# Norm stage of a four-layer kernel: turned pairs go round four PSUM banks in place of two, and ScalarE evacuates five of the eight pairs

## The chip, the cores and the metric

One NeuronCore of a Trainium2 chip. The metric is the device time of one execution in microseconds (us). Engines are called PE (TensorE, with its weight loads PEld), DVE (VectorE), ACT (ScalarE), POOL (GpSimd) and SP (SyncE, here the queue that issues most DMAs).

## What is computed

Two transformer layers on x of shape (2, 1024, 256), 2048 tokens in all, each sublayer behind a layer norm and with a residual:

```python
x = x + L0_attn(layernorm(x))      # 16 heads of 16, rotary embedding, causal
x = x + L0_ffn(layernorm(x))       # own norm with ln_weight, ln_bias; then @ sign(weight).T * max|weight| * gamma + beta
x = x + L1_attn(layernorm(x))      # 16 heads of 128, biases, causal
x = x + L1_ffn(layernorm(x))       # 64 experts, top 6 of 3 groups, capacity 96, plus a shared expert

def _layernorm(x, axis=-1, eps=1e-05):
    m = jnp.mean(x, axis=axis, keepdims=True)
    v = jnp.var(x, axis=axis, keepdims=True)
    return (x - m) / jnp.sqrt(v + eps)
```

The second norm is applied twice (the plain one and that of the feed-forward layer), in one pass.

## The kernel before, in words

The kernel is written by hand, engine by engine. x stays in SBUF as 16 tiles of 128 tokens x 256 (`g.x`). The program is a row of blocks. In a block each engine has its own list of instructions in the order written, semaphores join them, and a barrier of all engines ends the block: the next block begins when the last engine is through, SP's waits for its loads and stores included.

Four of these blocks are made by `norm` (line 164), one ahead of each sublayer:

- n0, ahead of the first attention. SP loads weights for the stages behind it.
- n1 (kind "ffn"), with a second level of statistics; its evacuation multiplies by `lnw` and adds `lnb`. No DMA.
- n2 (kind "split"), ahead of the second attention. The result is wanted as two f16 parts whose sum is the value: ScalarE copies the bank to `g.xs[0]` (line 274), VectorE subtracts that from the bank to `g.xs[1]` (line 257). SP loads 2.9 MB of weights.
- n3 (kind "keep"), ahead of the experts. SP also stores the normalized rows to DRAM (line 305).

Each norm has the same skeleton. VectorE computes mean and 1/std of all tiles in a chain of small operations, with one square root on ScalarE. Then it normalizes the 16 tiles one by one (line 249, 16 operations in 5.3 us) and signals each (`s_xn`). PE turns the tiles in eight pairs: a pair is two tiles of 128 tokens, and gives four 128x128 transposes (line 288) into one bank, of which the pair fills 512 f32 columns. A pair is then evacuated by two operations of 128x256 into the feature-major tensor `g.xT` (or `g.xs`). PE reuses a bank only when a semaphore says that it is empty.

Before the change the banks and the evacuating engines alternate together: pair p goes to bank p % 2, even pairs are evacuated by ScalarE (lines 202, 205), odd ones by VectorE (lines 197, 200). VectorE's evacuations stand behind its sixteen normalizing operations in its list. In n2 both engines work on every pair, and VectorE's subtraction frees the bank. PE waits so:

```python
for p in range(NT // 2):
    pe.wait_ge(s_xn, N0 + 2 * p + 2)
    if p >= 2:
        pe.wait_ge(s_ev[p % 2], N0 // 4 + p // 2)
```

The blocks behind the norms are: `l0_qkv` (line 371), where VectorE takes the maximum of a weight (`absmax`, line 334), POOL reduces it over the partitions (line 338) and then does an addition for each tile (line 441); `l0_ffn` (matmuls of line 1303); the second attention; and the router with the shared expert (matmuls of lines 1512 and 1525), whose SP queue begins the load of the expert weights.

Of the kernel before, what the change touches and what calls it, by code (L numbers as in the profile page):

```python
# [30 lines left out]
ACT = mybir.ActivationFunctionType  # L31
# [3 lines left out]
P = 128  # L35
B, S, D = 2, 1024, 256
T = B * S
NT = T // P
# [122 lines left out]
                dve.wait_ge(s_v, 3)  # L161


def norm(nc, g, tag, kind, loads=None, pool_work=None):


# [4 lines left out]

    s_sq, s_ch = [g.sem(f"{tag}_{n}") for n in ("sqrt", "chain")]
    s_st, s_ag, s_xn, s_tr = [g.sem(f"n_{n}") for n in ("stats", "aggr", "xn", "tr")]
    s_ev = [g.sem(f"n_evac{i}") for i in range(2)]

    N0 = int(tag[1]) * NT
    s_hi = g.sem(f"{tag}_hi") if kind == "split" else None
    s_kept = g.sem(f"{tag}_stored") if kind == "keep" else None
    with ExitStack() as c:
# [8 lines left out]
        with nc.Block() as block:  # L188
            def evac(eng, p):

                eng.wait_ge(s_tr, N0 // 2 + p + 1)
                for c_ in range(DC):
                    src = g.bank[p % 2][:, 0, c_ * 256:(c_ + 1) * 256]
                    dst = g.xT[:, c_, p * 256:(p + 1) * 256]
                    if p % 2:
                        if kind == "ffn":
                            ins = eng.tensor_scalar(dst, src, g.lnw[:, c_:c_ + 1], g.lnb[:, c_:c_ + 1],
                                                    ALU.mult, ALU.add)
                        else:
                            ins = eng.tensor_copy(dst, src)  # L200
                    elif kind == "ffn":
                        ins = eng.activation(dst, src, ACT.Identity, bias=g.lnb[:, c_:c_ + 1],
                                             scale=g.lnw[:, c_:c_ + 1])
                    else:
                        ins = eng.activation(dst, src, ACT.Copy)
                ins.then_inc(s_ev[p % 2], 1)

            @block.vector
            def _(dve):
                n = 0  # L210

                def chained(ins):

                    nonlocal n
                    n += 1
                    ins.then_inc(s_ch, 1)
                    dve.wait_ge(s_ch, n)

                if tag == "n0":
                    for t in range(NT):  # L220
                        dve.bn_stats(st[:, t, :], g.x[:, t, :]).then_inc(s_st, 1)
                for t in range(NT):
                    if tag == "n0":
                        dve.wait_ge(s_st, N0 + t + 1)
                    dve.bn_aggr(mv[:, t, :], st[:, t, :]).then_inc(s_ag, 1)
                dve.wait_ge(s_ag, N0 + NT)
                chained(dve.tensor_copy(g.mean[:, :], mv[:, :, 0]))
                chained(dve.tensor_copy(t1, mv[:, :, 1]))
                for lv in range(levels):
                    chained(dve.tensor_scalar(ve, t1, EPS, None, ALU.add))  # L230

                    dve.wait_ge(s_sq, lv + 1)
                    chained(dve.reciprocal(sq[:, :], sq[:, :]))
                    r = g.rstd[:, :]
                    one = sq[:, :]
                    chained(dve.tensor_tensor(t1, one, one, ALU.mult))
                    chained(dve.tensor_tensor(t1, t1, ve, ALU.mult))
                    chained(dve.tensor_scalar(t1, t1, -0.5, 1.5, ALU.mult, ALU.add))
                    if lv == 0:
                        chained(dve.tensor_tensor(r, one, t1, ALU.mult))  # L240
                    else:
                        chained(dve.tensor_tensor(one, one, t1, ALU.mult))
                        chained(dve.tensor_tensor(r, r, one, ALU.mult))
                    if lv + 1 < levels:

                        chained(dve.tensor_tensor(t1, r, r, ALU.mult))
                        chained(dve.tensor_tensor(t1, t1, mv[:, :, 1], ALU.mult))
                for t in range(NT):
                    dve.tensor_scalar(xn[:, t, :], g.x[:, t, :], g.mean[:, t:t + 1], g.rstd[:, t:t + 1],
                                      ALU.subtract, ALU.mult).then_inc(s_xn, 1)  # L250
                if kind == "split":
                    for p in range(NT // 2):

                        dve.wait_ge(s_hi, DC * (p + 1))
                        for c_ in range(DC):
                            cols = slice(p * 256, (p + 1) * 256)
                            ins = dve.tensor_tensor(g.xs[1][:, c_, cols], g.bank[p % 2][:, 0, c_ * 256:(c_ + 1) * 256],
                                                    g.xs[0][:, c_, cols], ALU.subtract)
                        ins.then_inc(s_ev[p % 2], 1)
                else:  # L260
                    for p in range(1, NT // 2, 2):
                        evac(dve, p)

            @block.scalar
            def _(act):
                for lv in range(levels):

                    act.wait_ge(s_ch, 3 if lv == 0 else 11)
                    act.activation(sq[:, :], ve, ACT.Sqrt).then_inc(s_sq, 1)
                if kind == "split":  # L270
                    for p in range(NT // 2):
                        act.wait_ge(s_tr, N0 // 2 + p + 1)
                        for c_ in range(DC):
                            act.activation(g.xs[0][:, c_, p * 256:(p + 1) * 256],
                                           g.bank[p % 2][:, 0, c_ * 256:(c_ + 1) * 256], ACT.Copy).then_inc(s_hi, 1)
                else:
                    for p in range(0, NT // 2, 2):
                        evac(act, p)

            @block.tensor  # L280
            def _(pe):
                for p in range(NT // 2):
                    pe.wait_ge(s_xn, N0 + 2 * p + 2)
                    if p >= 2:
                        pe.wait_ge(s_ev[p % 2], N0 // 4 + p // 2)
                    for c_ in range(DC):
                        for j in range(2):
                            ins = pe.transpose(g.bank[p % 2][:, 0, (2 * c_ + j) * P:(2 * c_ + j + 1) * P],
                                               xn[:, 2 * p + j, c_ * P:(c_ + 1) * P], g.identf[:, :])
                    ins.then_inc(s_tr, 1)  # L290

# [1742 lines left out]
```

## Time and profile before

| | us |
|---|---|
| median of 3 runs | 1579.84 |
| lowest, highest | 1574.81, 1579.88 |
| the profiled execution's own time | 1579.99 |
| its span in the trace | 1578.3 |

| engine | busy us | share of the span |
|---|---|---|
| PE | 1407.0 | 89% |
| DVE | 1050.9 | 67% |
| PEld | 985.8 | 62% |
| ACT | 813.1 | 52% |
| POOL | 375.3 | 24% |

The shares are averages over stages with different limits. The two attentions (96 to 382 us and 475.7 to 1240 us) keep PE nearly always busy; the norms lie between stages, at 10.9 to 31.5, 422 to 439, 457 to 475.4 and 1240 to 1255 us, and there no engine is busy all the time. How a stage is limited is read from its own rows, and in the norms from what the transposes wait for.

### The profile page before, as it was taken

To read this page: it belongs to the slowest core of one execution; us is meant where nothing else is said; L and a number is where in the kernel's file an instruction comes from. 1 tells how busy PE (TensorE), PEld (TensorE's weight loads), DVE (VectorE), ACT (ScalarE), POOL (GpSimd) and SP (SyncE) were. 2 spreads that over 40 slices of the span, in tenths; PEclk is the share of its full clock that TensorE was granted. 3 is DMA by queue.
4 is the path that set the end of the run, shared out by engine and by line. 5 is a ranking of instruction groups with operands and counts; after the bars stand their busy time and mean duration, and the time that the engine had idled before them with its cause. 6 is when DMAs were issued, how large, how long until landed. Compare 5 with 4: busy or idle time off the path is not lost. (4 is left out here: it accounts for less than half of the span.)

```text
span 1578.3 us, 36418 instructions
## 1 busy us (share of the span) xinstructions
PE 1407.0 (89%) x12869; PEld 985.8 (62%) x12869; DVE 1050.9 (67%) x2197; ACT 813.1 (52%) x1676; POOL 375.3 (24%) x796
## 2 busy tenths in 40 slices
PE   3848999998669999999979999999998798699977
PEld 2414555454555777777767677777777645599953
DVE  4766777775766888888841888888882368522229
ACT  1215656556216777777730787777781115333330
POOL 0344656430020111111120111111101000477730
PEclk9968999999869999999999999999999789799985
DMA  3027999972023755556540566556652340599948
GB/s 100 1 59 158 243 250 240 212 170 54 1 77 77 139 134 137 133 136 139 136 91 1 112 138 140 135 133 140 140 122 44 106 118 0 141 290 300 283 131 291
DMA packets 463402, 215.08 MB, mean 136 GB/s; under 512 B 412083, under 2 KB 434449, under 8 KB 463073
## 3 DMA queue, kind: packets, MB, share of 16 engines
q1 hardware_dynamic: 448992, 175.09, 46.9%
q0 software_dynamic: 12000, 36.90, 7.9%
q10 hardware_dynamic: 2336, 2.16, 0.4%
q8 instruction: 39, 0.64, 0.2%
q14 instruction: 35, 0.28, 0.1%
HBM read 81.97 MB, written 31.52 MB: 72 GB/s over the span
## 5 line engine op out<-in xcount | busy, mean ns | idle before, releaser
L1055 PE MATMUL bank<-a_pt,v_part 128*128 128x128 f16 x3456 | 234.2, 219 | 14.9 <-DMA a_pt<-a_ph 9.5
L737 DVE TENSOR_REDUCE a_qh<-bank 128x1 f16<-128x1024 f32 (+7 forms) x256 | 182.3, 755 | 86.5 <-PE bank L627 84.9
L1118 ACT ACTIVATE a_ph<-a_p,a_rinv 128x1024 f16<-128x1024 f32 (+7 forms) x256 | 198.6, 777 | 79.0 <-POOL a_rinv L997 76.0
L1055 PEld LDWEIGHTS bank<-a_pt,v_part 128*128 128x128 f16 x3456 | 207.7, 98 | 48.4 <-DMA a_pt<-a_ph 7.8
L1126 DVE TENSOR_REDUCE a_negm<-bank 128x1 f32<-128x1024 f32 (+7 forms) x256 | 191.8, 750 | 55.9 <-PE bank L1039 55.7
L1034 PE MATMUL bank<-a_k,a_q 128*128 128x512 f16 (+3 forms) x1152 | 228.6, 326 | 0.2
L725 ACT ACTIVATE a_p<-bank 128x1024 f32<-128x1024 f32 (+7 forms) x256 | 158.0, 650 | 129.8 <-PE bank L682 113.8
L1160 DVE SCALAR_TENSOR_TENSOR a_ph<-a_p,a_rinv,a_ph 128x1024 f16<-128x1024 f32 (+7 forms) x256 | 206.9, 808 | 1.7 <-ACT a_ph L1118 1.7
L1107 ACT ACTIVATE a_p<-bank,a_negm 128x1024 f32<-128x1024 f32 (+7 forms) x256 | 189.5, 740 | 21.6 <-DVE a_negm L1126 21.5
L997 POOL TENSOR_TENSOR a_rinv<-a_rinv,p_scale 128x1 f32<-128x1 f32 x256 | 49.0, 191 | 615.4 <-DVE a_rinv L1139 615.2
L906 PE MATMUL bank<-x_part,wsplit 128*128 128x512 f16 x768 | 187.3, 381 | 4.0 <-PEq L188 1.8
L624 PE MATMUL bank<-a_k,a_q 128*128 128x512 f16 (+3 forms) x384 | 109.5, 342 | 33.8 <-DMA a_k<-a_kh 19.4
L1034 PEld LDWEIGHTS bank<-a_k,a_q 128*128 128x128 f16 x1152 | 99.4, 98 | 60.6 <-ACT a_p L1107 1.2
L682 PE MATMUL bank<-a_qm,a_k 128*128 128x512 f16 (+3 forms) x384 | 113.0, 333 | 6.6 <-ACT a_p L725 5.2
L906 PEld LDWEIGHTS bank<-x_part,wsplit 128*128 128x128 f16 x768 | 70.1, 98 | 72.2 <-issue 5.6
L1742 POOL DMA_INDIRECT x_rows<-token_rows,src x64 | 63.1, 986 | 172.6 <-issue 170.2
L1793 PE MATMUL bank<-x_T,wgu 128*88 128x96 f32 x1024 | 96.4, 248 | 0.7 <-issue 0.7
L915 PE MATMUL bank<-wsplit,x_part 128*128 128x128 f16 x1536 | 95.9, 219 | 0.8 <-DVE a_k L941 0.5
L1793 PEld LDWEIGHTS bank<-x_T,wgu 128*88 128x88 f32 x1024 | 92.9, 158 | 4.5 <-issue 1.0
L915 PEld LDWEIGHTS bank<-wsplit,x_part 128*128 128x128 f16 x1536 | 88.2, 98 | 5.7 <-DVE a_k L941 2.1
L1911 DVE TENSOR_TENSOR x_h<-bank,x_sg 88x192 f32<-88x192 f32 x64 | 22.6, 354 | 94.8 <-ACT x_sg L1870 94.8
L1188 PE MATMUL bank<-wo_part,z_part 128*128 128x256 f16 x768 | 84.2, 273 | 1.7 <-PEq L966 1.7
(206 smaller groups left out, 2246.4 us busy)
## 6 DMA issues: line engine op xcount, KB each, us to landing
wgu<-in_wgu SPq DMA_DIRECT2D x64, 352.0 KB
choice_rows<-zero POOLq DMA_DIRECT2D x24, 512.0 KB, 5.2
c_rows<-choice_rows SPq DMA_DIRECT2D x16, 768.0 KB, 11.5
wsplit<-w_parts POOLq DMA_DIRECT2D x30, 384.0 KB, 3.9
wd<-in_wd SPq DMA_DIRECT2D x64, 176.0 KB
pw_in<-in_wqkv SPq DMA_DIRECT2D x16, 384.0 KB, 5.3
w_parts<-pw_part SPq DMA_DIRECT2D x16, 384.0 KB, 2.9
a_pt<-a_ph SPq DMA_TRANSPOSE x256, 3.0
```

What stands on the lines that cost most here:

```text
L682: ins = pe.matmul(ST[k % 2][:, c4 * 512:c4 * 512 + w_], kT[s][:, kb, :], queries[:, kb * P + c4 * 512:kb * P + c4 * 512 + w_], start=True, ...
L725: act.activation(pT[s][:, off[kb]:off[kb + 1]], ST[k % 2][:, 0:(BT - kb) * P], ACT.Exp).then_inc(e_ready, 1)
L737: dve.tensor_reduce(qh[s][:, i, MC:MC + 1], s1_place(t), AX.X, ALU.max, negate=True).then_inc(m_ready, 1)
L906: ins = pe.matmul(G_ps[k % 2], w[:, a, c_, (k // 2) * P:(k // 2 + 1) * P], g.xs[x_][:, c_, b * S + (k % 2) * 512:b * S + (k % 2 + 1) * 512 ...
L915: ins = pe.matmul(G_ps[k % 2][:, j * P:(j + 1) * P], g.xs[x_][:, c_, t * P:(t + 1) * P], w[:, a, c_, 2 * P:3 * P], start=(c_ == 0 and (a, ...
L1034: ins = eng.matmul(ps[:, c4 * 512:c4 * 512 + w_], qT[par][a][:, i * P:(i + 1) * P], kT[par][k_][:, c4 * 512:c4 * 512 + w_], start=(a, k_) ...
L1055: ins = eng.matmul(Z_ps[:, cols], g.vs[par][v_][:, k, :], turned[slot][:, a * blocks[j] + k, :], start=(k == 0 and (v_, a) == PARTS[0]), s ...
L1107: eng.activation(probs[j % NBUF][:, 0:w_], S_ps[j % 4][:, 0:w_], ACT.Exp, bias=negm[:, par, j:j + 1], accum_out=rsum[:, par, j:j + 1]).the ...
L1118: eng.activation(parts[slot][:, 0:w_], probs[slot][:, 0:w_], ACT.Copy, scale=rinv[:, p_, jj:jj + 1]).then_inc(p_hi, 1)
L1126: eng.tensor_reduce(negm[:, par, j:j + 1], S_ps[j % 4][:, 0:blocks[j] * P], AX.X, ALU.max, negate=True).then_inc(m_ready, 1)
L1160: eng.scalar_tensor_tensor(parts[slot][:, w_:2 * w_], probs[slot][:, 0:w_], rinv[:, p_, jj:jj + 1], parts[slot][:, 0:w_], ALU.mult, ALU.su ...
L1793: ins = pe.matmul(b_[:, m * C:(m + 1) * C], g.wgu[s][:, c_, m * MH:(m + 1) * MH], xeT[(s // 2) % 2][:, s % 2, c_, :], start=(c_ == 0), sto ...
```

## The change

`BY_DVE` lists the pairs that VectorE evacuates: 3, 5 and 7. ScalarE takes 0, 1, 2, 4 and 6. Pair p goes to bank p % 4. The semaphores `s_ev` now count by engine (0 ScalarE, 1 VectorE) and not by bank, and PE waits from pair 4 on, for the evacuation of pair p - 4. In the split norm both engines still work on every pair, and only the banks change.

```diff
@@ -161,6 +161,10 @@
                 dve.wait_ge(s_v, 3)
 
 
+BY_DVE = (3, 5, 7)
+
+
 def norm(nc, g, tag, kind, loads=None, pool_work=None):
 
 
@@ -171,9 +175,16 @@
 
     s_sq, s_ch = [g.sem(f"{tag}_{n}") for n in ("sqrt", "chain")]
     s_st, s_ag, s_xn, s_tr = [g.sem(f"n_{n}") for n in ("stats", "aggr", "xn", "tr")]
+
     s_ev = [g.sem(f"n_evac{i}") for i in range(2)]
 
     N0 = int(tag[1]) * NT
+    def earlier_norms(by):
+
+        each = len(BY_DVE) if by else NT // 2 - len(BY_DVE)
+        halves = 1 if int(tag[1]) == 3 else 0
+        return each * (int(tag[1]) - halves) + halves * by * (NT // 2)
+
     s_hi = g.sem(f"{tag}_hi") if kind == "split" else None
     s_kept = g.sem(f"{tag}_stored") if kind == "keep" else None
     with ExitStack() as c:
@@ -190,9 +201,9 @@
 
                 eng.wait_ge(s_tr, N0 // 2 + p + 1)
                 for c_ in range(DC):
-                    src = g.bank[p % 2][:, 0, c_ * 256:(c_ + 1) * 256]
+                    src = g.bank[p % 4][:, 0, c_ * 256:(c_ + 1) * 256]
                     dst = g.xT[:, c_, p * 256:(p + 1) * 256]
-                    if p % 2:
+                    if p in BY_DVE:
                         if kind == "ffn":
                             ins = eng.tensor_scalar(dst, src, g.lnw[:, c_:c_ + 1], g.lnb[:, c_:c_ + 1],
                                                     ALU.mult, ALU.add)
@@ -203,7 +214,13 @@
                                              scale=g.lnw[:, c_:c_ + 1])
                     else:
                         ins = eng.activation(dst, src, ACT.Copy)
-                ins.then_inc(s_ev[p % 2], 1)
+                ins.then_inc(s_ev[int(p in BY_DVE)], 1)
+
+            def evacuated(p):
+
+                by = int(kind == "split" or p in BY_DVE)
+                own = [q for q in range(p + 1) if kind == "split" or (q in BY_DVE) == bool(by)]
+                return s_ev[by], earlier_norms(by) + len(own)
 
             @block.vector
             def _(dve):
@@ -254,11 +271,11 @@
                         dve.wait_ge(s_hi, DC * (p + 1))
                         for c_ in range(DC):
                             cols = slice(p * 256, (p + 1) * 256)
-                            ins = dve.tensor_tensor(g.xs[1][:, c_, cols], g.bank[p % 2][:, 0, c_ * 256:(c_ + 1) * 256],
+                            ins = dve.tensor_tensor(g.xs[1][:, c_, cols], g.bank[p % 4][:, 0, c_ * 256:(c_ + 1) * 256],
                                                     g.xs[0][:, c_, cols], ALU.subtract)
-                        ins.then_inc(s_ev[p % 2], 1)
+                        ins.then_inc(s_ev[1], 1)
                 else:
-                    for p in range(1, NT // 2, 2):
+                    for p in BY_DVE:
                         evac(dve, p)
 
             @block.scalar
@@ -272,20 +289,21 @@
                         act.wait_ge(s_tr, N0 // 2 + p + 1)
                         for c_ in range(DC):
                             act.activation(g.xs[0][:, c_, p * 256:(p + 1) * 256],
-                                           g.bank[p % 2][:, 0, c_ * 256:(c_ + 1) * 256], ACT.Copy).then_inc(s_hi, 1)
+                                           g.bank[p % 4][:, 0, c_ * 256:(c_ + 1) * 256], ACT.Copy).then_inc(s_hi, 1)
                 else:
-                    for p in range(0, NT // 2, 2):
-                        evac(act, p)
+                    for p in range(NT // 2):
+                        if p not in BY_DVE:
+                            evac(act, p)
 
             @block.tensor
             def _(pe):
                 for p in range(NT // 2):
                     pe.wait_ge(s_xn, N0 + 2 * p + 2)
-                    if p >= 2:
-                        pe.wait_ge(s_ev[p % 2], N0 // 4 + p // 2)
+                    if p >= 4:
+                        pe.wait_ge(*evacuated(p - 4))
                     for c_ in range(DC):
                         for j in range(2):
-                            ins = pe.transpose(g.bank[p % 2][:, 0, (2 * c_ + j) * P:(2 * c_ + j + 1) * P],
+                            ins = pe.transpose(g.bank[p % 4][:, 0, (2 * c_ + j) * P:(2 * c_ + j + 1) * P],
                                                xn[:, 2 * p + j, c_ * P:(c_ + 1) * P], g.identf[:, :])
                     ins.then_inc(s_tr, 1)
 
```

PE's list in n0, before (identf is the identity, n0_xnb the normalized tiles; n_xn counts those tiles, n_evac0 and n_evac1 the evacuations):

```order
L288 MATMUL bank0<-identf,n0_xnb 128x128 [waits n_xn]
L288 MATMUL bank0<-identf,n0_xnb 128x128 x3
L288 MATMUL bank1<-identf,n0_xnb 128x128 [waits n_xn]
L288 MATMUL bank1<-identf,n0_xnb 128x128 x3
L288 MATMUL bank0<-identf,n0_xnb 128x128 [waits n_evac0,n_xn]
L288 MATMUL bank0<-identf,n0_xnb 128x128 x3
L288 MATMUL bank1<-identf,n0_xnb 128x128 [waits n_evac1,n_xn]
L288 MATMUL bank1<-identf,n0_xnb 128x128 x3
L288 MATMUL bank0<-identf,n0_xnb 128x128 [waits n_evac0,n_xn]
L288 MATMUL bank0<-identf,n0_xnb 128x128 x3
L288 MATMUL bank1<-identf,n0_xnb 128x128 [waits n_evac1,n_xn]
L288 MATMUL bank1<-identf,n0_xnb 128x128 x3
```

And now:

```order
L306 MATMUL bank0<-identf,n0_xnb 128x128 [waits n_xn]
L306 MATMUL bank0<-identf,n0_xnb 128x128 x3
L306 MATMUL bank1<-identf,n0_xnb 128x128 [waits n_xn]
L306 MATMUL bank1<-identf,n0_xnb 128x128 x3
L306 MATMUL bank2<-identf,n0_xnb 128x128 [waits n_xn]
L306 MATMUL bank2<-identf,n0_xnb 128x128 x3
L306 MATMUL bank3<-identf,n0_xnb 128x128 [waits n_xn]
L306 MATMUL bank3<-identf,n0_xnb 128x128 x3
L306 MATMUL bank0<-identf,n0_xnb 128x128 [waits n_evac0,n_xn]
L306 MATMUL bank0<-identf,n0_xnb 128x128 x3
L306 MATMUL bank1<-identf,n0_xnb 128x128 [waits n_evac0,n_xn]
L306 MATMUL bank1<-identf,n0_xnb 128x128 x3
```

Pairs 2 and 3 (third and fourth row pair) go to banks of their own and lose their wait for an evacuation; pair 4 (fifth) now waits for pair 0, and pair 5 for pair 1, both of ScalarE.

VectorE's evacuations stand in its list in n0 as eight copies out of bank 1; of the change they are these, up to the end of the block:

```order
L211 COPY xT0<-bank3 128x256 [waits n_tr]
L211 COPY xT0<-bank3 128x256
L211 COPY xT0<-bank1 128x256 [waits n_tr]
L211 COPY xT0<-bank1 128x256
L211 COPY xT0<-bank3 128x256 [waits n_tr]
L211 COPY xT0<-bank3 128x256
```

The copies of pair 1 are gone from here to ScalarE's list, and the first that VectorE makes is now that of pair 3. In ScalarE's list in n0 stand now:

```order
L216 ACTIVATE xT0<-bank0 128x256 [waits n_tr]
L216 ACTIVATE xT0<-bank0 128x256
L216 ACTIVATE xT0<-bank1 128x256 [waits n_tr]
L216 ACTIVATE xT0<-bank1 128x256
L216 ACTIVATE xT0<-bank2 128x256 [waits n_tr]
L216 ACTIVATE xT0<-bank2 128x256
L216 ACTIVATE xT0<-bank0 128x256 [waits n_tr]
L216 ACTIVATE xT0<-bank0 128x256
L216 ACTIVATE xT0<-bank2 128x256 [waits n_tr]
L216 ACTIVATE xT0<-bank2 128x256
```

Before, ScalarE had four pairs there, all out of bank 0.

## Rows read from the trace of the kernel before

**Rows 1.** What PE sat idle before the transposes of L288 until (us, times).
```profile
  DVE x_part L257: 4.9, 3
  DVE xT L200: 4.5, 2
  DVE xT_ffn L197: 3.2, 3
```

**Rows 2.** Four turning stretches: start:end length, PE PEld DVE ACT POOL busy, PEclk, DMA share, GB/s.
```profile
20.27:31.48 11.21, 8.01 (x32) 6.09 (x32) 7.39 (x22) 2.63 (x8) 0.00 (x0) 1.00 0.04 9
427.22:438.94 11.72, 7.15 (x32) 5.43 (x32) 8.36 (x22) 4.08 (x8) 0.00 (x0) 0.65 0.01 2
461.22:475.38 14.16, 7.79 (x32) 6.00 (x32) 10.35 (x30) 5.26 (x16) 0.68 (x2) 0.50 0.41 150
1244.15:1254.91 10.76, 7.50 (x32) 5.80 (x32) 7.40 (x22) 2.64 (x8) 0.00 (x0) 0.58 0.56 195
```

**Rows 3.** Timeline of the first norm: start us, us, engine, line, op, [idle before <-releaser].
```profile
20.27 3.04 PE L288 MATMUL bank<-identf,n_xnb 128*128 128x128 f32 x12 [20.27 <-DVE n_xnb L249]
...
21.42 0.66 ACT L205 ACTIVATE xT<-bank 128x256 f32<-128x256 f32 x2 [3.17 <-PE bank L288]
...
23.34 0.66 ACT L205 ACTIVATE xT<-bank 128x256 f32<-128x256 f32 x2 [1.27 <-PE bank L288]
...
24.66 0.74 DVE L200 COPY xT<-bank 128x256 f32<-128x256 f32 x2
...
25.55 5.14 PE L288 MATMUL bank<-identf,n_xnb 128*128 128x128 f32 x20 [2.24 <-DVE xT L200]
...
30.72 0.76 DVE L200 COPY xT<-bank 128x256 f32<-128x256 f32 x2 [1.27 <-PE bank L288]
...
31.80 0.69 DVE L334 TENSOR_REDUCE fw_am<-fw_w 128x1 f32<-128x512 f32 x1 [0.33 <-PEq L188]
```

**Rows 4.** Timeline of the second norm (n1).
```profile
428.38 1.02 ACT L202 ACTIVATE xT_ffn<-bank,lnb,lnw 128x256 f32<-128x256 f32 x2 [3.38 <-PE bank L288]
...
431.61 0.99 DVE L197 TENSOR_SCALAR xT_ffn<-bank,lnw,lnb 128x256 f32<-128x256 f32 x2
...
432.74 1.07 PE L288 MATMUL bank<-identf,n_xnb 128*128 128x128 f32 x8 [2.12 <-DVE xT_ffn L197]
```

**Rows 5.** Timeline of the third norm (n2, the split one).
```profile
465.64 1.40 DVE L257 TENSOR_TENSOR x_part<-bank,x_part 128x256 f16<-128x256 f32 x4
...
466.53 1.94 PE L288 MATMUL bank<-identf,n_xnb 128*128 128x128 f32 x8 [3.34 <-DVE x_part L257]
...
473.77 1.61 DVE L257 TENSOR_TENSOR x_part<-bank,x_part 128x256 f16<-128x256 f32 x4 [1.11 <-ACT x_part L274]
...
473.94 0.66 ACT L274 ACTIVATE x_part<-bank 128x256 f16<-128x256 f32 x2 [0.20 <-PE bank L288]
```

**Rows 6.** Two single microseconds, in the third and in the fourth norm, columns as Rows 2.
```profile
469.00:470.00 1.00, 0.75 (x4) 0.71 (x4) 0.86 (x3) 0.17 (x1) 0.00 (x0) 0.50 0.02 8
...
1252.00:1253.00 1.00, 1.00 (x7) 0.95 (x5) 0.42 (x2) 0.07 (x1) 0.00 (x0) 0.50 0.00 0
```

**Rows 7.** Timeline of POOL in the stage after the first norm.
```profile
37.91 0.38 POOL L338 PARTITION_ALL_REDUCE fw_am<-fw_am  x1 [36.08 <-issue]
...
45.44 2.48 POOL L441 TENSOR_TENSOR rot<-rot 128x512 f32<-128x512 f32 x2 [7.15 <-issue]
```

**Rows 8.** One microsecond of the second norm, columns as Rows 2.
```profile
433.00:434.00 1.00, 0.81 (x8) 0.57 (x6) 0.59 (x2) 0.15 (x1) 0.00 (x0) 0.97 0.00 0
```

**Rows 9.** Timeline, matmuls of the feed-forward stage after the second norm.
```profile
439.26 8.06 PE L1303 MATMUL bank<-wf,xT_ffn 128*128 128x256 f32 x25 [1.36 <-PEq L188]
...
444.79 10.96 PE L1303 MATMUL bank<-wf,xT_ffn 128*128 128x256 f32 x50
```

**Rows 10.** The router and shared-expert stage after the fourth norm, columns as Rows 2.
```profile
1267.90:1320.00 52.10, 44.43 (x96) 18.03 (x96) 39.23 (x148) 13.46 (x29) 0.00 (x0) 0.93 0.20 60
```


## Prediction

> **What bounds the kernel now.** The change touches only the four norms, so I looked first at what TensorE (PE) waits for before the transposes of line 288. [rows 1] says it waits 4.9, 4.5 and 3.2 us for the evacuations that VectorE makes (copies out of the banks): 12.6 us in eight waits. These are waits for a free bank, not for data. (It also waits for the first normalized rows of each norm; the change cannot touch that.) Next I cut the trace into the four stretches from the first transpose of a norm to its last evacuation [rows 2]: 11.21, 11.72, 14.16 and 10.76 us, 47.85 in all. PE is busy for only 7.15 to 8.01 us of each, and no other engine fills its stretch. Nothing overlaps a norm from outside: each is a block with a barrier at its end, so what a stretch loses, the program should lose.
>
> The timeline shows why [rows 3]. PE turns three pairs in 3.04 us, then stands still for 2.24 us. Pair 3 wants the bank of pair 1, pair 1 is VectorE's to empty, and VectorE's queue holds the sixteen normalizing operations first; it comes to its first copy at 24.66. ScalarE meanwhile has nothing to do. From 25.55 PE works through five pairs in 5.14 us and VectorE's last copy ends the stretch at 31.48.
>
> **First norm.** The change adds no work: the same 32 transposes and 16 copies. One pair of copies goes from VectorE (0.74 us) to ScalarE (0.66 us). Pairs 0 to 3 have their own banks. ScalarE's copies of pair 0 and 2 begin at 21.42 and 23.34, so two pairs are 1.92 us apart: 0.96 per pair, and a pair's copy can begin 1.15 us after its first transpose (21.42 - 20.27). With no wait the transposes of pair 7 begin at 20.27 + 7 x 0.96 = 26.99, its data are there at 28.14, and VectorE's copy (0.76) ends at 28.90. No wait takes the old one's place: ScalarE has pairs 0 to 2 out by 24.00, PE wants their banks at 24.11, 25.07 and 26.03. Pair 3's bank is empty at 24.66 + 0.74 = 25.40, and wanted at 26.99. 31.48 - 28.90 = **2.6 us**.
>
> **Second norm.** Its copies scale and shift, and cost about 1.0 us a pair on either engine [rows 4]. Pair 2 may now begin at once. ScalarE: pair 0 from 428.38 to 429.40, pair 1 to 430.45, pair 2 to 431.47, always before PE wants the bank (431.06, 432.02, 432.98). VectorE starts at 431.61 with pair 3. Pair 7 begins at 427.22 + 6.72 = 433.94, is there at 435.10, and is copied by 436.09. 438.94 - 436.09 = **2.8 us** at the lower clock; the upper end is a rival below.
>
> **Third norm.** The halves are made by both engines: ScalarE copies, VectorE subtracts, and VectorE empties every bank. So pair 4 still waits for VectorE's subtraction of pair 0, which begins at 465.64; PE starts pair 4 at about 466.5, as it starts pair 2 now [rows 5]. But four pairs and not two are then turned and copied, so VectorE goes through pairs 0 to 3 with no gap (two pairs in 1.40 us) until 468.44, while PE turns 4 to 7 behind it: pair 7 begins at 466.50 + 3 x 0.96 = 469.38, is there at 470.53, ScalarE's copy (0.66) ends at 471.19, and VectorE ends 0.78 us after that, as it does now for pair 7 (ScalarE from 473.94 to 474.60, VectorE until 475.38): 472.0. 475.38 - 472.0 = **3.4 us**. The loads that this block waits for must be in by then. The DMA engines are at 0.02 of their time by 469 [rows 6], 3 us earlier; the cover of this term is thereby 3 us, no more.
>
> **Fourth norm.** Same copies as the first, so the same length, 28.90 - 20.27 = 8.63 us, against 10.76: **2.1 us**. This block also stores the normalized rows. DMA share is 0.00 from 1252.0 on [rows 6], and my new end is 1244.15 + 8.63 = 1252.8. That is just enough; had the stores finished later, this term would shrink one for one.
>
> **Sum.** 2.6 + 2.8 + 3.4 + 2.1 = 10.9, with the second decimals 11.0 us. The profiled execution took 1579.99 us (span 1578.3) and the median is 1579.84, so the two stand within 0.2 us and I forecast 1580.0 - 11.0 = **1569.0 us**. The ceiling by [rows 1] is 12.6 us, the floor for a norm is 0 where something else ends the block; the waits removed cannot be worth less than nothing. A run of the kernel before has also been 5 us below the median, so 2 us of scatter go on either side.
>
> **A rule of the Trainium skill on the clock.** [rows 8] shows transposes at granted clock 0.97, that is 2.4 GHz, where in the microseconds before PE had done nothing but transposes; [rows 4] shows what it is worth: eight in 1.07 us, against eight in 1.94 at 1.2 GHz [rows 5]. The Trainium skill (TensorE: Matmul & The Clock Gate, Part 4: PE-mode transpose) holds that transposes do not count as activity for the clock gate and the full clock does not engage for them. By that rule the norms would stay at the lower level, which is what my sum assumes; by the rows the higher level can come, and the sum could grow as in the first rival. The measurement decides, so the rival stays open.
>
> **Rival 1: the clock rises earlier.** PE now works with fewer gaps, so the grant may come within a norm and last into the next stage. In the second norm only VectorE would then bound: 431.61 + 3 x 0.99 = 434.6, another 1.5 us. After it the feed-forward matmuls run 0.32 us each (8.06 / 25) before the rise and 0.22 (10.96 / 50) after it [rows 9]; if 15 of the 25 slow ones became fast, that is 1.5 us. A like amount may come in the first matmuls after the third norm. For: the fast patch of [rows 8]. Against: in the first norm five pairs without a gap stayed at 0.26 us a transpose (5.14 / 20). (The clock column reads 1.00 there [rows 2], but the durations are those of the lower level; I go by the durations.) About 4 us more: **1565 us**.
>
> **Rival 2: the first norm's gain is swallowed.** The next stage waits for POOL. VectorE's maximum ends at 31.80 + 0.69 = 32.49 [rows 3], POOL's all-reduce starts only at 37.91, and its first addition at 45.44 [rows 7], both with a wait that the profile calls issue. If these 13 us hang on that maximum, they move with it; if they end at a fixed time from the kernel's start, 2.6 us are lost: **1571.6 us**. I hold the first likelier: the all-reduce is written behind a wait for that maximum, and no transfer or other event in the rows ends at 37.9.
>
> **Rival 3: given back.** PE stops earlier in the norms, the clock falls sooner, and the stages behind start at 1.2 GHz for longer; or the store or the loads turn out to end the fourth or third block. Two lost terms or 3 to 5 us of slow matmuls: about **1574 us**.
>
> **Rival 4: slower.** One mechanism, in the router and shared-expert stage behind the fourth norm, where PE is busy 44.4 of 52.1 us at a mean clock of 0.93 [rows 10]. If the changed phase left PE at 1.2 GHz through it, its 44.4 us would become 44.4 x 0.93 / 0.50 = 82.6, 38 us more, and the kernel would take 1569 + 38 = **1607 us**. It decides from the point where 11.0 + 7.9 = 18.9 us are added, about half of that stage. Against it: the clock did come back there before, after the same stretch of small matmuls, and the change does not touch them.
>
> That the change doesn't do what it says is excluded by the order of instructions: pair 4 is the first to wait for an evacuation, in each norm.
>
> **How the numbers follow.** Forecast 0.55, rival 1 0.15, rival 2 0.12, rival 3 0.15, rival 4 0.03. A measurement of this kernel can tell 0.5% from no change, that is 7.9 us: 1571.9. Forecast with its scatter is faster in most cases (0.48 of 0.55), rival 1 always (0.15), rival 2 a little less than half (0.05), rival 3 hardly: 0.68 faster, 0.28 same, 0.04 slower. The range takes in forecast, rivals 1 and 2 and the near part of 3: 1563.5 to 1573.5.
>
> **What would show it.** In the profile after: PE's waits for VectorE's evacuations at the transposes near 1 us in all (pair 4 of the third norm alone) in place of 12.6; the four stretches 8.6, 8.9, 10.8 and 8.6 us; ScalarE's first three pairs 0.96 us apart; the all-reduce at 35.3 and not at 37.9. Wrong would be stretches of this length with a time above 1574 (then a later stage gave it back, and its windows will say which), or stretches ended by a DMA.

## The result, and the profile after

The changed kernel takes 1560.86 us in the median of 4 runs (1557.80 to 1564.13), the kernel before 1579.86 in the same session. The ratio is 0.9878 with a 95% interval of 0.985 to 0.9905: 19.0 us less. I had forecast 11.0 us less, with a range of 1563.5 to 1573.5: the result lies 2.6 us below it. The direction was right and the size too small: 11.0 of the 19.0. The profiled execution of the changed kernel took 1557.80 us (span 1556.1), that of the kernel before 1579.99, so the two traces differ by 22.2 us, 3 more than the medians do.

First the four stretches from a norm's first transpose to its last evacuation, which answer to [rows 2] (columns as there):

```profile
20.01:26.71 6.70, 5.26 (x32) 4.81 (x32) 6.54 (x20) 3.29 (x10) 0.00 (x0) 1.00 0.02 3
419.57:427.25 7.68, 6.64 (x32) 6.40 (x32) 7.37 (x20) 4.88 (x10) 0.00 (x0) 0.61 0.01 3
447.09:457.53 10.44, 7.32 (x32) 6.54 (x32) 10.14 (x30) 5.27 (x16) 0.58 (x2) 0.56 0.53 206
1225.38:1232.69 7.31, 6.50 (x32) 6.27 (x32) 6.65 (x20) 3.29 (x10) 0.00 (x0) 0.61 0.78 268
```

They took 11.21, 11.72, 14.16 and 10.76 us and take 6.70, 7.68, 10.44 and 7.31: 15.7 us less. I had said 8.6, 8.9, 10.8 and 8.6, that is 11.0 less. What PE waits for before its transposes, which answers to [rows 1] (us, times):

```profile
  DVE x_part L274: 1.6, 1
  DVE xT L211: 0.6, 1
```

2.2 us in two waits in place of 12.6 in eight. The mechanism is the forecast one, and it is in the timeline of the first norm, which answers to [rows 3]:

```profile
20.01 4.63 PE L306 MATMUL bank<-identf,n_xnb 128*128 128x128 f32 x28 [20.01 <-DVE n_xnb L266]
...
21.16 0.66 ACT L216 ACTIVATE xT<-bank 128x256 f32<-128x256 f32 x2 [3.17 <-PE bank L306]
...
22.01 0.66 ACT L216 ACTIVATE xT<-bank 128x256 f32<-128x256 f32 x2 [0.20 <-PE bank L306]
...
22.87 0.66 ACT L216 ACTIVATE xT<-bank 128x256 f32<-128x256 f32 x2 [0.20 <-PE bank L306]
23.80 0.66 ACT L216 ACTIVATE xT<-bank 128x256 f32<-128x256 f32 x2 [0.28 <-PE bank L306]
24.39 1.41 DVE L211 COPY xT<-bank 128x256 f32<-128x256 f32 x4
24.68 0.66 ACT L216 ACTIVATE xT<-bank 128x256 f32<-128x256 f32 x2 [0.21 <-PE bank L306]
...
25.29 0.63 PE L306 MATMUL bank<-identf,n_xnb 128*128 128x128 f32 x4 [0.65 <-DVE xT L211]
...
25.95 0.76 DVE L211 COPY xT<-bank 128x256 f32<-128x256 f32 x2 [0.15 <-PE bank L306]
```

Seven pairs, 28 transposes, follow one another without a wait; ScalarE's first copies begin at 21.16, 22.01 and 22.87, **0.85 us apart and not 0.96**; VectorE comes free at 24.39 and finds two pairs ready. The one wait left (0.65 us) is pair 7 for pair 3's bank. The clock rose inside the seven: ScalarE's copies of pairs 4 and 6 begin 0.88 us apart, 0.44 us a pair, half of 0.85, and pair 7 takes 0.63 us where a pair alone took 1.0 and more. (The clock column reads 1.00 throughout this stretch, so the two levels are told apart by the durations.) At 0.85 the seven pairs would take about 6.0 us, an estimate; they took 4.63.

The fourth norm shows a term that I had on the edge (the last line is of the waits of SP, us in total, times, longest):

```profile
1225.38 6.50 PE L306 MATMUL bank<-identf,xn 128*128 128x128 f32 x32 [5.79 <-DVE xn L266]
...
1231.93 0.76 DVE L211 COPY xT<-bank 128x256 f32<-128x256 f32 x2 [0.37 <-PE bank L306]
...
1234.03 13.40 PE L1530 MATMUL bank<-gate,xT 128*128 128x64 f32 x64 [2.14 <-PEq L199]
...
SPq L199 <- DMA token_rows<-xn: 3.3, 1, 3.3
```

VectorE is through at 1232.69, 0.33 us after which the next stage would begin; it begins at 1234.03, because SP still waits 3.3 us for the stores of the normalized rows. Of the 3.45 us that the stretch lost, 1.03 came back there. The four norms together give 15.7 - 1.0 = 14.7 us.

Behind the norms stages are shorter or longer in which no instruction changed. To see it I set, for every trace, the times between the first instructions of the stages side by side (worked out from the starts of instructions; in us):

| stage | before | before, again | after | after, again |
|---|---|---|---|---|
| norm 1 stretch | 11.21 | 11.21 | 6.70 | 6.69 |
| first attention | 292.20 | 292.20 | 290.90 | 290.59 |
| its output projection | 22.87 | 22.79 | 21.19 | 21.20 |
| norm 2 stretch | 11.72 | 11.73 | 7.67 | 7.18 |
| feed-forward | 17.90 | 17.98 | 15.47 | 15.47 |
| norm 3 stretch | 14.16 | 14.16 | 10.44 | 10.04 |
| start of the second attention | 14.90 | 14.91 | 13.64 | 14.99 |
| rest of the second attention | 749.49 | 749.11 | 749.84 | 749.56 |
| norm 4 stretch | 10.75 | 10.79 | 7.30 | 7.31 |
| its end to the router's start | 0.32 | 0.32 | 1.35 | 1.32 |
| router matmuls | 12.47 | 12.10 | 13.19 | 13.17 |
| shared expert | 47.12 | 45.81 | 46.36 | 46.39 |
| experts and combination | 222.77 | 224.37 | 222.30 | 222.09 |

The rows leave out short stretches that differ by 0.7 us in all. The 7.5 us that remain of the 22.2 are in the feed-forward (2.4), the output projection (1.7), the first attention (1.3), the start of the second (1.3), and some tenths elsewhere; the router costs 0.7 more. "Again" is a second profile of the same kernel, from the experiments: of the 1.3 at the start of the second attention nothing is left there.

The feed-forward stage after, which answers to [rows 9], is at the granted clock of 1.00 from its first matmul (PEclk is the column before the last two); before, its mean was 0.86:

```profile
427.57:443.04 15.47, 14.05 (x64) 12.06 (x64) 12.12 (x33) 0.00 (x0) 11.03 (x18) 1.00 0.00 0
```

### The profile page after: what moved, and what is told of

It is laid out like the page before. It is cut to its first block and busy times, and to the rows that moved or that the text cites. A ratio compares the mean times of both kernels' runs of the same rounds, so it can differ in the third digit from the quotient of the medians.

```text
span 1556.1 us, 36410 instructions
## 1 busy us (share of the span) xinstructions
PE 1394.1 (90%) x12869; PEld 982.9 (63%) x12869; DVE 1047.9 (67%) x2191; ACT 814.5 (52%) x1682; POOL 374.1 (24%) x796
```

## The experiments

Twelve kernels ran, the two of the change and ten variants. In the diffs FILL, BANKS and BY_DVES are tables by norm, so that one norm can be changed alone. Where a norm is "filled", PE turns the identity into half a bank that nobody reads, while it would stand idle; nothing else is added, and all outputs are computed as before.

### Which part of the change does it: banks, split, or how many banks

Banks alone:

```diff
-BY_DVES = ((3, 5, 7),) * 4
+BY_DVES = ((1, 3, 5, 7),) * 4      # BANKS stays (4, 4, 4, 4)
```

> Edit: four banks as in the change, but the pairs alternate between the engines as before (VectorE 1, 3, 5, 7). Theory A (the waits for a bank were the cost, and PE turns a pair in 0.85 us when no bank holds it): the first norm's stretch from first transpose to last evacuation goes from 11.2 to 7.5-8.8 us, the second's to about 8.5, the third's to 10.4 (nothing differs from the change there), the fourth's to 7.5-8.8; with the feed-forward stage starting at the full clock the kernel takes 1564 to 1567. Theory B (the split between the engines is what counts): the first norm stays above 10 us, and only the third gains; about 1575.

The split alone:

```diff
-BANKS = (4, 4, 4, 4)
+BANKS = (2, 2, 2, 2)               # BY_DVES stays ((3, 5, 7),) * 4
```

> Edit: ScalarE takes pairs 0, 1, 2, 4, 6 and VectorE 3, 5, 7, but in two banks. Theory A: PE waits at every pair for a bank of the pair two before; the first norm's stretch is about 9.2 us in place of 11.2, the second and fourth gain about 2 us each, the third nothing; about 1574. Theory B: nearly the whole gain of the change, about 1563.

Three banks:

```diff
-BANKS = (4, 4, 4, 4)
+BANKS = (3, 3, 3, 3)
```

> Edit: the changed kernel with three banks in place of four. Theory A: the first norm loses 0.3 to 0.7 us (pair 6 waits for VectorE's pair 3), the third about 0.9, the second up to 0.5, the fourth is hidden by its stores; with the stages behind unchanged about 1563. If the gain needs four banks, the stretches go back half way to two banks (9 and 12.3 us): 1569.

Measured:

| kernel | median us | ratio, 95% interval | the four stretches, us | sum |
|---|---|---|---|---|
| before | 1579.3 to 1580.4 in three sessions | | 11.21, 11.72, 14.16, 10.75 | 47.8 |
| split alone | 1570.51 | 0.9941, 0.9918 to 0.9964 | 8.27, 8.99, 14.16, 8.27 | 39.7 |
| banks alone | 1559.38 | 0.9889, 0.9866 to 0.9911 | 7.58, 9.35, 10.42, 7.58 | 34.9 |
| three banks, split | 1563.51 | 0.9897, 0.9873 to 0.9921 | 7.14, 7.62, 10.96, 7.14 | 32.9 |
| four banks, split (the change) | 1560.86 | 0.9878, 0.9850 to 0.9905 | 6.70, 7.67, 10.44, 7.30 | 32.1 |
| the change again | 1561.82 | 0.9888, 0.9856 to 0.9921 | 6.69, 7.18, 10.04, 7.31 | 31.2 |

The banks bring 12.9 us of the 15.7, the split the last 2.8; alone the split would bring 8.1, for the two cure in part the same waits. The third norm tells them apart: the split does nothing there (14.16), the banks all. Of the banks, the third brings nearly everything: with the split, the sum goes from 39.7 with two banks to 32.9 with three and 32.1 with four. In the time the split's 2.8 us can't be seen: banks alone ran as fast as the whole change, and so 5 to 8 us faster than I had expected of it. Where its trace made them up is told below, with the clock. The split alone did better than expected too (first norm 8.27 us and not 9.2, time 1570.5 and not 1574), three banks as expected. First the waits. With the split alone, the first norm (timeline):

```profile
20.21 4.88 PE L313 MATMUL bank<-identf,n_xnb 128*128 128x128 f32 x20 [20.21 <-DVE n_xnb L273]
...
23.29 0.66 ACT L223 ACTIVATE xT<-bank 128x256 f32<-128x256 f32 x2 [0.41 <-PE bank L313]
...
25.49 1.07 PE L313 MATMUL bank<-identf,n_xnb 128*128 128x128 f32 x8 [0.40 <-DVE xT L218]
```

PE is not stopped by VectorE for the first five pairs, but ScalarE's third copy begins 1.08 us after its second where unhindered pairs are 0.85 apart: the third pair waited for ScalarE to empty bank 0. The two steps together are 1.93 us, the 1.92 that I had read from the kernel before as the rate of two free pairs. With banks alone:

```profile
20.08 4.22 PE L313 MATMUL bank<-identf,n_xnb 128*128 128x128 f32 x20 [20.08 <-DVE n_xnb L273]
...
25.36 1.51 PE L313 MATMUL bank<-identf,n_xnb 128*128 128x128 f32 x12 [1.05 <-DVE xT L218]
```

five pairs in one go, then 1.05 us of waiting for VectorE's copy of pair 1. With three banks the wait stands in front of pair 6, for VectorE's copy of pair 3:

```profile
20.04 4.65 PE L313 MATMUL bank<-identf,n_xnb 128*128 128x128 f32 x24 [20.04 <-DVE n_xnb L273]
...
25.32 1.06 PE L313 MATMUL bank<-identf,n_xnb 128*128 128x128 f32 x8 [0.63 <-DVE xT L218]
```

### The change in the second norm alone

```diff
-BANKS = (2, 2, 2, 2); BY_DVES = ((1, 3, 5, 7),) * 4
+BANKS = (2, 4, 2, 2); BY_DVES = ((1, 3, 5, 7), (3, 5, 7), (1, 3, 5, 7), (1, 3, 5, 7))
```

> Edit: the change in the second norm alone (four banks, VectorE 3, 5, 7); the other norms as before. Theory A with the clock carried over: the norm's stretch is 7.7 us in place of 11.7 and the feed-forward stage behind it (first matmul to last statistics) 15.2 in place of 17.6, since it begins at 2.4 GHz: 6.4 us, about 1573.5; all other stages as before. Rival: the feed-forward gain belongs to scatter and not to the norm: 4.0 us, about 1576, with the stage at 17.6.

1576.20 us, ratio 0.9976 (0.9958 to 0.9993). The norm's stretch is 7.62 us and the feed-forward stage 15.47, both as the first theory has them: 6.5 us. The whole gained only 3 us. In its trace 6.7 us are given back: the start of the second attention takes 15.96 us (14.90 before), its rest 751.17 (749.49), router and shared expert 62.6 together (59.6), POOL's part of the stage behind the first norm 49.1 (48.1). Another 2.3 us are gained ahead of the edit, in the first norm (10.75 for 11.21), the first attention (290.68 for 292.20) and its output projection (22.54 for 22.87). So the gain inside the norm is in the trace, and stages without an edit, behind it and ahead of it, move by as much, in either direction.

### The kernels before and after, unchanged, once more

> The kernel before, unchanged, for a second profile of it. If the first attention (31.8 to 427.2 us in the trace shown) is 395.4 us again within 0.5 us, its 2.9 us in the changed kernel need a cause; if it moves by 2 us or more by itself, they are scatter. The third norm and the stages behind the others should repeat within 0.3 us.

> The changed kernel, unchanged, for a second profile and more runs. The four stretches repeat within 0.1 us (6.7, 7.7, 10.4, 7.3), except where the clock rises at another moment; the router stage is 13.2 or 7.2 us by the clock at its start. Whole 1561.

The kernel before took 1578.41 us, the changed one 1561.82 (ratio 0.9888, 0.9856 to 0.9921). The table above has their stages. Each kernel repeats most of its stages to 0.1 us, at this clock or that; the exceptions are 0.2 to 1.6 us. So the 1.3 us of the first attention are not plain scatter between executions, as I had thought possible. But in the other profiles that stage takes from 290.4 to 292.7 us, with the norms of before and with those of after, so it can't be put down to the four banks either.

### The same work, 2.6 us later

```diff
                 if tag == "n0":
+                    for i in range(6):
+                        dve.bn_stats(tmp[:, 0, 0:6], g.x[:, 0, :]).then_inc(g.sem("delay"), 1)
+                        dve.wait_ge(g.sem("delay"), i + 1)
                     for t in range(NT):
```

> Edit: the kernel before with six more statistics operations of VectorE ahead of those of the first norm, each waited for: all that follows starts some 2.5 us later, and no work behind it differs. If the clock's moments are bound to the program, every stage has its old length and the whole is 1582.3. If they run apart from it, stages that start at a low clock change their length (feed-forward 15.5 or 17.9, router 7.2 or 12.5, output projection 21.2 or 22.9) with no work changed, and the whole differs from 1582.3 by some us either way.

1585.93 us against 1580.44, ratio 1.0039 (1.0023 to 1.0054): 5.5 us more, of which 2.6 are the shift. In the trace (4.1 us longer) feed-forward takes 18.02 us, router 12.64, the third norm 14.16: as before. The output projection takes 23.85 (22.87), the second norm 12.18 (11.72), the first 10.76 (11.21). The answer lies between the two theories: the clock's moments mostly move with the program, but not wholly, and a shift of 2.6 us with no other change costs 3 us more in the median (1.0 to 5.9 by the interval). So a change of that size behind a norm can come from nothing but the time at which a stage starts.

### Is it the clock, behind the norms?

The second norm filled in the kernel before, with its two banks and its waits:

```diff
+FILL = {'n1': (28, 8)}
...
+                def fill(count):
+                    for _ in range(count):
+                        pe.transpose(g.bank[3][:, 1, 0:P], g.identf[:, :], g.identf[:, :])
+                head, tail = FILL.get(tag, (0, 0))
+                fill(head)
                 for p in range(NT // 2):
...
+                fill(tail)
```

> Edit: the kernel before, with the filler in the second norm, 28 ahead and 8 behind; two banks as before. If the clock alone is behind the faster feed-forward stage, that stage takes 15.5 us in place of 17.9 although the norm still waits for banks; the norm itself shortens only by PE's part, from 11.7 to about 10.7. Whole about 1576. If the feed-forward stage stays at 17.9, its gain in the change has another cause.

1580.06 us, ratio 0.9990 (0.9968 to 1.0012): no difference. Two windows of its trace, the norm's pairs and the feed-forward stage:

```profile
426.00:436.00 10.00, 6.89 (x31) 5.25 (x30) 6.96 (x19) 3.68 (x8) 0.00 (x0) 0.54 0.00 0
...
437.60:453.00 15.40, 14.05 (x64) 12.10 (x64) 12.13 (x32) 0.00 (x0) 11.00 (x16) 1.00 0.00 0
```

The feed-forward runs at 1.00 throughout and takes 15.47 us, although the norm is as slow as before (11.72, where I had expected 10.7: the filler ran at full clock, and the pairs behind it came at 0.54 all the same). So the short feed-forward stage does not need the four banks; it needs the clock. But this isn't a clean proof that keeping PE busy brings it: the next kernel, whose second norm is untouched, has 15.47 us there too. I can say that the stage takes 15.5 us where the granted clock is 1.00 at its start and 16.9 (banks alone) to 18.0 where it is 0.50 there, and that all eight profiles in which VectorE takes three pairs of this norm, with two, three or four banks, show 15.47. Why the kernel before is at 17.9 to 18.0 in three profiles of three, that one included which starts 2.6 us later, stays open.

The fourth norm, filled in the kernel before (FILL = {'n3': (18, 8)}) and in the changed one ({'n3': (18, 28)}):

> Edit: the kernel before, and in the fourth norm PE turns the identity into an unused half bank, 18 times ahead of the first pair and 8 times behind the last. Theory C (the clock granted at the router's first narrow matmul decides that stage: at 2.4 GHz it holds, below it is not reached again until the wide matmuls): the stage from the first router matmul to the first shared-expert matmul takes 7.2 us in place of 12.1 to 12.5, the whole about 5 us less, 1574. Rival: that stage has its length from something else (in the run with banks only it was 7.2 by another cause): 12.1 to 12.5 again, the whole 1579.

> Edit: the changed kernel with the same filler in the fourth norm, 18 ahead and 28 behind (PE stands idle there for 2.2 us now). Theory C: router stage 7.2 us in place of 13.2, whole about 1554.5. Rival: 1560.9, as the changed kernel. If the filler runs at 1.2 GHz, its tail delays the end of the block by up to 4 us and the kernel is slower than the changed one.

In the kernel before, 1571.94 us, ratio 0.9956 (0.9934 to 0.9978): 7 to 8 us less with no bank and no evacuation changed. Its trace has 8.3 us less in router and shared expert; it also has the short feed-forward stage and an output projection of 21.19 us, both of which run ahead of the filler, so not every difference in it is the filler's. PE at the end of the norm and in the router:

```profile
1251.11 1.56 PE L287 MATMUL bank<-identf 128*128 128x128 f32 x8
...
1253.06 7.33 PE L1522 MATMUL bank<-gate,xT 128*128 128x64 f32 x64 [0.39 <-PEq L191]
```

64 router matmuls in 7.33 us, as in the run with banks alone and against 12.68 in the kernel before. What decides is whether the full clock holds into the stage: it was there at the router's first matmul in the kernel before too, and fell 1.3 us later. So theory C, by which the clock at the first matmul decides, is wrong in that form. In the changed kernel PE stood at full clock when the last pair was turned, then idle for 2.14 us, and the clock fell 0.5 us after the router began (three microseconds of the trace after):

```profile
1231.00:1232.00 1.00, 0.89 (x7) 0.65 (x6) 0.63 (x3) 0.51 (x2) 0.00 (x0) 0.93 1.00 352
...
1233.00:1234.00 1.00, 0.00 (x0) 0.00 (x1) 0.00 (x0) 0.01 (x1) 0.00 (x0) 1.00 0.09 29
...
1235.00:1236.00 1.00, 1.00 (x7) 1.00 (x6) 0.00 (x0) 0.28 (x1) 0.00 (x0) 0.50 0.77 197
```

The router's matmuls (64 columns each) keep PE busy all the time and still run at 1.2 GHz to the end of the stage, and the shared expert's begin at it. In the run with banks alone the clock rose 3.7 us before the router's first matmul (2.9 in the changed kernel), PE was idle for 1.85 us, and it held; which of the two counts isn't shown:

```profile
1240.00:1241.00 1.00, 1.00 (x11) 1.00 (x11) 0.21 (x1) 0.58 (x1) 0.00 (x0) 1.00 0.83 152
...
1243.00:1244.00 1.00, 1.00 (x11) 1.00 (x11) 0.00 (x0) 0.00 (x0) 0.00 (x0) 1.00 0.94 257
```

11 matmuls touch a microsecond there, 7 above. That gave this kernel 8.2 us in router (7.17) and shared expert (44.16) against the change, and hides the 2.8 us that its norms are slower and the 1.4 that it loses in its feed-forward stage. The time by itself would have said that the split is worth nothing.

In the changed kernel with 18 and 28 turns of the identity: 1559.54 us, ratio 0.9872 (0.9836 to 0.9908), not told apart from the change. The router was quick, but the filler itself was in the way:

```profile
1236.68 3.22 PE L305 MATMUL bank<-identf 128*128 128x128 f32 x28
...
1240.62 7.33 PE L1540 MATMUL bank<-gate,xT 128*128 128x64 f32 x64 [0.71 <-PEq L202]
```

PE went on turning 2.3 us past the last evacuation (1237.6) and held up the barrier, at 2.98 us from the norm's end to the router's start in place of 1.35.

### A shorter filler, and the stores out of the way

> Edit: the changed kernel, and behind the last pair of the fourth norm PE turns the identity 16 times into an unused half bank, in the 2.2 us in which it now stands idle until the barrier. Theory C: the full clock that comes with the last pairs holds over the barrier, the router stage takes 7.2 us and not 13.2, the shared expert 44.2 and not 46.4, and nothing is delayed: whole about 1554. Rival: no effect, 1561.

> Edit: as the last, with 10 turns of the identity, and SP waits for the stores of the normalized rows at the end of the next block and not of the norm's. The block's end then follows the last evacuation by 0.3 us and not 1.35: 1 us more than the run with the tail alone, about 1553. If the router's first loads on the same queue hold it up, nothing is gained by it.

```diff
-FILL = {}
+FILL = {'n3': (0, 16)}             # the first; (0, 10) in the second
...
-                    sp.wait_ge(s_kept, 64)
...
# the second: at the end of SP's list in the router's block
+            sp.wait_ge(g.sem("n3_stored"), 64)
```

With the short filler alone: 1555.80 us (1550.97 to 1564.57 in six runs), ratio 0.9836 (0.9811 to 0.9862). Its profile is of its slowest run, and there the effect failed: the router began at full clock and lost it in the middle of the stage,

```profile
1239.00:1240.00 1.00, 1.00 (x11) 1.00 (x11) 0.31 (x3) 0.78 (x1) 0.00 (x0) 1.00 0.64 101
...
1243.00:1244.00 1.00, 1.00 (x7) 1.00 (x6) 0.00 (x0) 0.00 (x0) 0.00 (x0) 0.50 0.93 287
```

with 11.34 us for it. So a full clock at the start isn't enough. PE had been idle for 0.98 us ahead of the stage; that this cost the clock isn't shown, since with banks alone it held over 1.85.

With the stores' wait moved as well: **1554.33 us**, ratio 0.9830 (0.9808 to 0.9851), and its six runs lie within 4 us of each other (1551.52 to 1555.43), where those of the changed kernel spread over 6 to 10. The router starts 0.60 us after the last evacuation, and PE stands idle for 0.30 us only before it:

```profile
1234.53 1.26 PE L305 MATMUL bank<-identf 128*128 128x128 f32 x10
...
1236.09 7.33 PE L1540 MATMUL bank<-gate,xT 128*128 128x64 f32 x64 [0.30 <-PEq L202]
```

This is the lowest median of all, 6.5 us below the changed kernel, whose interval (from 0.9850, and from 0.9856 when it ran again) begins where this one's ends. The short filler alone is not told apart from it by the intervals, and the two differ in the filler's length as well, so what moving the wait brings by itself is not shown.

## Why the prediction was right or wrong

**The 8.0 us between forecast and result.** The norms were worth 14.7 us and not 11.0: 2.6 more by the rate of a pair, 2.1 more by the clock inside them, 1.0 less by the stores. The other 4.3 (19.0 - 14.7, in the medians) came from the stages behind, which my sum put at nothing. The rate alone would have made 1566.4 us, inside my range; what took the result below it was the clock in the norms and the stages behind them.

**What bounds the norms: right.** The waits were for banks, behind VectorE's queue, and they are gone (12.6 to 2.2 us). The wait that I said would stay is the one that stayed: pair 4 of the third norm, now for 1.6 us. The order of the four gains is not the forecast one: I had the third norm as the largest, and it is the first. My ceiling of 12.6 us was none: the stretches lost 15.7, since the ceiling counted only the waits in [rows 1], not the shorter waits for ScalarE's banks and not the clock.

**The rate of a pair: the first step that failed.** I wrote: "ScalarE's copies of pair 0 and 2 begin at 21.42 and 23.34, so two pairs are 1.92 us apart: 0.96 per pair". Between the two lay a bank wait of its own: pair 2 wanted bank 0, which ScalarE emptied at 21.42 + 0.66 = 22.08. Unhindered pairs are 0.85 us apart in every trace with spare banks. It could have been read: 8 transposes take 1.94 us in [rows 5] and 12 take 3.04 in [rows 3], so the third pair cost 1.10 and a pair without a wait costs less. With 0.853 in place of 0.96 my own working gives 7.9, 8.1, 10.4 and 7.9 us, 2.6 us less in all. I took the rate of a stage from a stretch that the removed resource already limited.

**The clock, in the norms and behind them: the second step that failed.** My sum held every norm at 1.2 GHz and every stage behind at its old length; the rest was left to a rival. The other 2.1 us by which the stretches beat the forecast are pairs turned at 2.4 GHz (pair 7 of the first norm in 0.63 us). I held against this that five pairs without a gap had stayed slow in the kernel before (5.14 us). They were not without a gap: at 0.85 a pair they would take about 4.5, an estimate with the last pair's 1.06; the rest was waiting for banks. And the same unchanged first norm took 10.75 us in three later profiles (the change in the second norm alone, the two fillers in the kernel before), in place of 11.21: in them the clock rose inside it. Of the Trainium skill's rule (TensorE: Matmul & The Clock Gate, Part 4: PE-mode transpose) that transposes do not count for the clock: for these f32 transposes with the identity it does not hold. In the first norm after, pair 7 took 0.63 us, and PE had done nothing but transposes in this execution until then. The same holds for the fourth norm, where the clock stands at 0.50 until 1231 and at 1.00 by 1233, and PE had run transposes alone from 1225.38 on.

**The fourth norm's stores: the margin was named, and used up.** "That is just enough; had the stores finished later, this term would shrink one for one." The stores did not finish later; the evacuations finished earlier, at 7.3 us and not 8.6, and the surplus of 1.0 us was lost. The router starts 8.65 us after the norm's first transpose; by my forecast it would have been 8.63 + 0.32 = 8.95, so the margin was 0.3 us. Term by term: 4.5 (forecast 2.6), 4.0 (2.8), 3.7 (3.4), 2.4 (2.1).

**Rival 1: half right, and too small.** I gave the stages behind the norms 1.5 us and "a like amount", 3 us; in the profiles they brought 7.5, in the medians 4.3. The feed-forward term alone was 2.4, by the clock at its start. Output projection and first attention (3.0) I had not in the list, and the experiments do not bind them to the change: the projection takes 21.19 us also where only the fourth norm is filled, and 22.87 with three banks. So what makes up the 4.3, beyond the feed-forward stage, stays open. That rival 1's 1565 is nearer the result than the forecast is in part luck, since it has neither the rate nor these two stages.

**Rival 2: false.** POOL's work moved with the block (after, answering to [rows 7]):

```profile
32.85 0.38 POOL L356 PARTITION_ALL_REDUCE fw_am<-fw_am  x1 [31.02 <-issue]
...
40.63 2.48 POOL L459 TENSOR_TENSOR rot<-rot 128x512 f32<-128x512 f32 x2 [7.40 <-issue]
```

The maximum starts at 27.03, the all-reduce 5.8 us behind it (6.1 before), the first addition 13.6 us behind it (13.6 before). Of the 4.8 us, 4.7 came through to the end of that stage (POOL's last addition ends at 88.86 and not at 93.54).

**Rival 3** had the right place (stores, and slow matmuls in the stages behind), and both occurred: 1.0 us and 0.7 us. **Rival 4** did not occur in the change; its place, the router, turned out to be worth 6 to 8 us either way, not 38.

**The range** was built on terms at one clock and one rate, and on 2 us of scatter. The kernel before spreads over 13 to 16 us in a session (1572.8 to 1586.1, 1574.9 to 1591.0). The ends should have had the case in which the rate and the clock are better together.

## What to carry to other kernels

To forecast what more buffers bring, take the rate of a step from a place where no buffer is waited for; two instructions with a copy between them are no such place. In a program of short stages between barriers, where PE drops to 1.2 GHz in the gaps, a change of a few us moves the clock's state in the stages behind it by as much; so compare stage by stage, and take the same kernel's second profile before a difference is given a cause. In this kernel the gap ahead of the router was worth filling, and the filler has to end before the barrier would.

## What the runs showed of the hardware that was not expected

The router's 64 matmuls of 64 columns keep PE busy without a gap and take 7.2 us where the granted clock stays at 2.4 GHz, 11.3 to 13.7 where it falls to 1.2. Nine of the ten traces with the long stage had 2.4 GHz at its first matmul and fell within the next microseconds (one just before), and in none of the ten did these matmuls bring it back; it rose again 2.2 to 5.2 us after the shared expert's matmuls had begun. It stayed up in four traces, with PE idle for 0.30, 0.39, 0.71 and 1.85 us ahead of the stage, and was lost in ten with 0.98 to 2.29 us. So the three shortest idle times all kept it, and of the eleven from 0.98 us up one did. Three of the four that kept it also had the filler in the norm, and that the idle time is the cause is not shown. The change does not touch this stage, and it is worth 6 us, with the shared expert behind it up to 8.
